# A recommendation tower on one core: GpSimd's gathers in two gated runs per tile, and the two gram fills side by side

## The chip, the cores and the metric

The kernel runs on one core of one Trainium2 chip. The metric is the device time of one execution in microseconds (us), lower is better; where several runs are given, their median is meant. The engines are called PE (TensorE, matrix products), DVE (VectorE), ACT (ScalarE), POOL (GpSimd, which here issues the indirect gathers) and SP (SyncE, which issues the plain transfers).

## What is computed

A batch of 2048 samples has 26 ids each and a dense vector of 128 numbers. Each id picks a row of 128 numbers from its table (1000 to 125000 rows). All pairs of the 27 vectors are multiplied, and the products go with the dense vector through three layers.

```
e = stack([tbl_f[ids[:, f]] for f in range(26)], axis=1)      # 2048 x 26 x 128
sd = einsum('bfd,bd->bf', e, dense)                           # 26 dot products
ss = einsum('bfd,bgd->bfg', e, e); pairs = ss[:, iu, ju]      # 325 dot products
h = concatenate([dense, sd, pairs, dense], axis=1)            # 2048 x 607
h = maximum(h @ W_top1 + b_top1, 0)                           # 512
h = maximum(h @ W_top2 + b_top2, 0)                           # 256
y = h @ W_top3                                                # 2048 x 1
```

Everything is float32.

## The kernel before

**Tiles and steps.** The 2048 samples are 16 tiles of 128. Two tiles make a step, d = tile // 2 and t = tile % 2, so there are eight steps.

**Two ways to fetch a row.** Nine small tables (`ONEHOT`) are never gathered. Their rows are looked up with matrix products: DVE writes a one-hot matrix (`set_pack`, L346), PE multiplies it by the table, which lies in SBUF split in a high and a low part (`lookup`, L592; in the first step three tables are used whole, L588). One table takes two "packs" of a step, of four products by two parts each, so a pack is 8 matmuls. Nine tables are 18 packs a step, nine in each of its two sections. In steps 3, 5 and 7 (`TEN_STEPS`) table 0 is looked up as well: 20 packs. The other tables are gathered by POOL, one indirect DMA of 128 rows for each table and tile (L311). Their 17 gathers are in groups j = 0 to 4 of 4, 4, 4, 4 and 1; a tile of the steps 3, 5 and 7 has 16 gathers and no group 4. In all 266 gathers. They land in `rows`, which has two halves, so that tile T+2 writes where tile T was.

**What is done with them.** PE transposes a group (`transpose_rows`, L605) and ACT copies it into `vecT` (`drain_rows`, L426); ACT copies a looked-up table there too (`drain_sum`, L418). When all 27 vectors of a tile are in `vecT`, PE fills two PSUM banks with the dot products of every sample with small matmuls, 64 for each half: `gram(tile, 0)` and `gram(tile, 1)`, L619, the "gram fills". ACT copies them out (`drain_gram`, L435), DVE turns and sorts them (`turn`, L356 and L362), PE transposes the result (`transpose_pairs`, L633), and then come layers 1 to 3 (L640 and L644, L653, L659).

**The order.** Every engine's order is written out by hand. On PE tile T has a "section": its gram fills first, with layer work of the step before and the first packs of the step after between them; then more packs, and after packs 2, 4, 5, 7 and 8 (counted from 0) the transposes of the groups 0 to 4 of tile T+1. A section with t = 0 holds layer 1 (three of its four parts) and half of layer 2; a section with t = 1 the rest of layer 2, layer 3 and the first part of layer 1. The first step's 18 packs stand before all sections, with the transposes of tile 0 after packs 3, 6, 9, 12 and 13. The last two tiles have an order of their own, which the change does not touch.

**The semaphores that matter.** `vec_filled` counts PE's fills of the two vector banks (transposed groups and gram halves), and `pack_done` counts the packs that PE has finished. POOL waits, before group j of tile T+2, until PE has transposed group j of tile T (the buffer is free then), and before group 3 also for both gram halves of tile T.

Of the kernel before, what the change touches and what calls it, by code (L numbers as in the profile page):

```python
# [18 lines left out]
LOOKED_UP = ONEHOT + [SOMETIMES]  # L19
TEN_STEPS = [3, 5, 7]  # L20
LATE_SPLIT = 4
GRAM_AHEAD_OF = 3
SPLIT_AT_FIRST = len(LOOKED_UP) - LATE_SPLIT


# [33 lines left out]
def build(nc, dense_t, ids, ids_t, tables, weights, y):  # L59
# [3 lines left out]
    TD = 2  # L63
# [32 lines left out]
    X_AFTER = 7  # L96
    LATE_LOW_AT = {2 * n: SPLIT_AT_FIRST + n for n in range(LATE_SPLIT)}
    SUM_AFTER = 5

    STEP_USES = TD + M1 + M2 + 1  # L100

# [3 lines left out]
    def sum_at(d, q):  # L105
        return sum(NH[:d]) + q

    def pack_at(d, p):
        return PER * sum_at(d, 0) + p

    def half_packs(d):
        return PER * NH[d] // TD if d < STEPS else PER * NH[0] // TD

    def groups(tile):
        return GROUPS - (tile // TD in TEN_STEPS)

    def rows_at(tile, j):
        return sum(groups(n) + 2 for n in range(tile)) + j

    def gram_at(tile, h):  # L120
        return rows_at(tile, groups(tile)) + h

    def same_rows(tile, j):
        return [n for n in range(tile % TD, tile, TD) if j < groups(n)]
# [16 lines left out]
    def layer3_at(d):  # L141
        return STEP_USES * (d + 1) - (d == STEPS - 2)
# [10 lines left out]
    def group(j):  # L153
        return GATHERED[FG * j:FG * (j + 1)]
# [4 lines left out]
    with ctx:  # L159
# [6 lines left out]
        def sem(name):  # L166
            return ctx.enter_context(nc.semaphore(name))
# [77 lines left out]
        vec_filled, vec_drained = sem("vec_filled"), sem("vec_drained")  # L245
# [6 lines left out]
        pack_set, pack_done = sem("pack_set"), sem("pack_done")  # L252
# [40 lines left out]
        @block.gpsimd  # L293
        def _(pool):
            nc.gpsimd.memset(ident[:], 0.0).then_inc(ident_zero, 1)
            for c in heights:
                nc.gpsimd.iota(row_i[c][:], pattern=[[1, c]], base=0, channel_multiplier=c
                               ).then_inc(rows_numbered, 1)
            pool.wait_ge(ident_zero, 1)
            nc.gpsimd.affine_select(out=ident[:], in_=ident[:], compare_op=ALU.not_equal, fill=1.0, base=0,  # L300
                                    pattern=[[-1, P]], channel_multiplier=1).then_inc(ident_set, 1)

            pool.wait_ge(ids_loaded, 16)
            for tile in range(TILES):
                for j in range(groups(tile)):
                    if tile >= TD:
                        pool.wait_ge(vec_filled, rows_at(same_rows(tile, j)[-1], j) + 1)
                    if tile >= TD and j == GRAM_AHEAD_OF:
                        pool.wait_ge(vec_filled, gram_at(tile - TD, 1) + 1)
                    for n, f in enumerate(group(j)):  # L310
                        nc.gpsimd.indirect_dma_start(  # L311
                            rows[:, tile % TD, FG * j + n, :], None, tables[f],
                            bass.IndirectOffsetOnAxis(ids_all[:, tile, f:f + 1], 0)
                        ).then_inc(gathered[tile % TD][j], 16)

        @block.vector
        def _(dve):
# [59 lines left out]
            for tile in range(TILES):  # L377
                d, t = tile // TD, tile % TD
                for k in range(half_packs(d + 1)):
# [4 lines left out]
                    if k == TURN_AFTER:  # L384
                        turn(tile)
                    if tile == 1 and k == SUM_AFTER:
                        dve.wait_ge(weights_loaded, 16)
# [4 lines left out]
        def _(act):  # L392
# [37 lines left out]
            def drain_gram(tile, h):  # L430
                use = gram_at(tile, h)
                if h == 0 and tile:
                    act.wait_ge(tile_turned, tile)
                act.wait_ge(vec_filled, use + 1)
                nc.scalar.copy(dots[:, h * HALF:(h + 1) * HALF, :],  # L435
                               vec_bank[use % 2][:, 0:HALF * GC].rearrange("p (i f) -> p i f", f=GC)
                               ).then_inc(vec_drained, 1)
# [15 lines left out]
            def drain_layer1(d, m):  # L453
                drain_unit(layer1_at(d, m), h1, m, b1_sb, 0, DS)

            def drain_layer2(d, m):
                drain_unit(layer2_at(d, m), h2, m, b2_sb, 0, DS)

            def drain_y(use, d, t0, nt):
                act.wait_ge(work_filled, use + 1)  # L460
                nc.scalar.copy(y_by_tile[:, TD * d + t0:TD * d + t0 + nt, :],
                               work_bank[use % 2][:, 0:nt * BL].rearrange("p (t i) -> p t i", t=nt)
                               ).then_inc(work_drained, 1)
# [22 lines left out]
            for tile in range(TILES - 2):  # L486
                d, t = tile // TD, tile % TD
                for h in range(2):
                    drain_gram(tile, h)
                    if t == 0 and d:  # L490
                        drain_layer1(d - 1, 1 + h)
                    if t == 1 and d and h == 0:
                        drain_layer2(d - 1, 1)
                    if t == 1 and d and h == 1:
                        drain_y(layer3_at(d - 1), d - 1, 0, TD)
                    drain_table(d + 1, half_packs(d + 1) * t + h)
                    if tile == 0 and h + 2 < LATE_SPLIT:
                        copy_whole(SPLIT_AT_FIRST + h + 2)
                        set_late_high(SPLIT_AT_FIRST + h + 2)
                for k in range(2, half_packs(d + 1)):  # L500
                    drain_table(d + 1, half_packs(d + 1) * t + k)
                    if k in ROWS_AFTER and ROWS_AFTER[k] < groups(tile + 1):
                        drain_rows(tile + 1, ROWS_AFTER[k])
                    if t == 0 and d and k == LATE_LAYER1_AFTER:
                        drain_layer1(d - 1, M1 - 1)
                    if k == PAIRS_AFTER:
                        drain_pairs(tile)
                    if t == 0 and d + 1 < STEPS and k == X_AFTER:
                        copy_x(d + 1)
                if t == 0 and d:  # L510
                    drain_layer2(d - 1, 0)
                if t == 1:
                    drain_layer1(d, 0)
# [10 lines left out]
            d = STEPS - 1  # L524
# [34 lines left out]
        def _(pe):  # L559
# [36 lines left out]
            def free_vec(use):  # L596
                if use >= 2:
                    pe.wait_ge(vec_drained, use - 1)
# [10 lines left out]
            def gram(tile, h):  # L609
                into = gram_at(tile, h)  # L610
                if h == 0:
                    pe.wait_ge(sum_drained, sum_at(tile // TD + 1, 0))
                    pe.wait_ge(x_copied, tile // TD + 1)
                    pe.wait_ge(vec_drained, rows_at(tile, groups(tile) - 1) + 1)
                free_vec(into)
                for i in range(HALF):
                    for j in range(4):
                        s = BL * j + h * HALF + i
                        last = nc.tensor.matmul(vec_bank[into % 2][BL * j:BL * j + GC, i * GC:(i + 1) * GC],  # L619
                                                vecT[:, slot(tile), s, 0:GC], vecT[:, slot(tile), s, 1:VECS],  # L620
                                                start=True, stop=True)
                last.then_inc(vec_filled, 1)
# [71 lines left out]
            for tile in range(TILES - 2):  # L694
                d, t = tile // TD, tile % TD
                for h in range(2):
                    gram(tile, h)
                    if t == 0 and d:
                        layer1(d - 1, 1 + h)
                    if t == 1 and d and h == 0:  # L700
                        layer2(d - 1, 1)
                    if t == 1 and d and h == 1:
                        layer3(d - 1)
                    table_step(d + 1, half_packs(d + 1) * t + h)
                for k in range(2, half_packs(d + 1)):
                    table_step(d + 1, half_packs(d + 1) * t + k)
                    if k in ROWS_AFTER and ROWS_AFTER[k] < groups(tile + 1):
                        transpose_rows(tile + 1, ROWS_AFTER[k])
                    if t == 0 and d and k == LATE_LAYER1_AFTER:
                        layer1(d - 1, M1 - 1)  # L710
                    if k == PAIRS_AFTER:
                        transpose_pairs(tile)
                if t == 0 and d:
                    layer2(d - 1, 0)
                if t == 1:
                    if d == 0:
                        pe.wait_ge(w1x_summed, 1)
                    layer1(d, 0)
# [22 lines left out]
            d = STEPS - 1  # L741
# [77 lines left out]
```

## Time and profile before

| | |
|---|---|
| median of 3 timed runs | 369.42 us (369.02 to 369.57) |
| span of the profiled execution | 543.7 us |
| PE busy in it | 392.0 us |
| POOL busy in it | 253.7 us |
| DVE busy in it | 233.2 us |
| ACT busy in it | 186.9 us |
| mean granted TensorE clock in it | 0.836 |

The page gives the span, from the first to the last instruction, and no time for what lies before and behind it. The profiled execution is 174 us longer than the timed ones, so its durations of single instructions can be used, while its waits have to be looked at one by one. In a timeline a row stands for neighbouring instructions of one kind: start, duration, engine, line, operation, count, and in brackets the idle time ahead with what ended it. "x8" of L592 is one pack. A float32 product of layers 1 to 3 counts as two.

### The profile page before, as it was taken

How to read it: one execution, taken by the hardware profiler on the slowest of the kernel's cores; microseconds unless marked ns; L12 is line 12 of the kernel's file. 1: busy time of each engine (PE TensorE's matmuls, PEld its weight loads, DVE VectorE, ACT ScalarE, POOL GpSimd, SP SyncE). 2: the span in 40 equal slices, each digit the busy share in tenths (PEclk: the TensorE clock that was granted, in tenths of full speed). 3: DMA queues.
4: the chain of work that ended last, by engine and by line, in shares of the span. 5: the costliest groups of instructions: out<-in, count | busy, mean ns of one | idle time of the engine just before them, and what ended most of it. 6: DMA issues, size and time to landing. Idle time of an engine off the chain costs nothing.

```text
span 543.7 us, 13728 instructions
## 1 busy us (share of the span) xinstructions
PE 392.0 (72%) x6224; PEld 342.7 (63%) x6224; DVE 233.2 (43%) x324; ACT 186.9 (34%) x283; POOL 253.7 (47%) x273
## 2 busy tenths in 40 slices
PE   5631776283986829876896959967795956969987
PEld 3520775272875718766685938857684934859876
DVE  6310887271461523635353533716454432555202
ACT  0110773231442323422324324513434313344453
POOL 6775627265263742627265363626465371552000
PEclk9955798595897958989797868979798885989999
DMA  8725105011020110201011011211112010110000
GB/s 229 204 54 128 30 20 190 26 41 43 12 59 26 46 39 17 59 21 53 23 41 53 24 43 28 58 27 45 35 41 54 20 51 17 40 49 22 2 4 2
DMA packets 11755, 26.84 MB, mean 49 GB/s; under 512 B 4652, under 2 KB 5804, under 8 KB 11570
## 3 DMA queue, kind: packets, MB, share of 16 engines
q0 software_dynamic: 8512, 17.45, 12.3%
q1 hardware_dynamic: 3186, 8.52, 5.5%
q8 instruction: 49, 0.80, 0.6%
q14 instruction: 8, 0.07, 0.0%
HBM read 25.95 MB, written 0.01 MB: 48 GB/s over the span
## 4 chain that ended last, share of the span: by engine, by line
PE 58%; another core or an unknown queue 24%; issue 10%; ACT 8%
PE sum_bank L592 22%; PE vec_bank L619 9%; PE work L644 8%; PE work L653 6%; PE vec_bank L605 5%; ACT vecT L426 4%; PE work L640 3%; ACT vecT L418 2%; PE id_bank L566 1%; PE work L633 1%; PE work L729 1%; PE work L659 0%; ACT parts L395 0%; ACT late L442 0%
## 5 line engine op out<-in xcount | busy, mean ns | idle before, releaser
L311 POOL DMA_INDIRECT rows<-in_tbl,ids_all x266 | 252.9, 951 | 245.6 <-PE vec_bank L619 143.8
L346 DVE TENSOR_TENSOR onehot<-id_bank,row_f 125x1024 fp32r<-125x1024 f32 x150 | 177.0, 1217 | 256.4 <-remote 133.7
L592 PE MATMUL sum_bank<-onehot,parts 125*128 125x256 f32 x1152 | 187.8, 306 | 54.3 <-issue 34.5
L592 PEld LDWEIGHTS sum_bank<-onehot,parts 125*128 125x128 f32 x1152 | 164.5, 204 | 67.4 <-issue 57.9
L426 ACT COPY vecT<-vec_bank 128x512 f32<-128x512 f32 (+1 forms) x74 | 83.2, 1128 | 82.1 <-remote 66.0
L418 ACT COPY vecT<-sum_bank 128x256 f32<-128x256 f32 x75 | 52.5, 700 | 118.0 <-remote 76.4
L619 PE MATMUL vec_bank<-vecT 128*26 128x26 f32 x4096 | 51.8, 200 | 45.8 <-issue 29.8
L619 PEld LDWEIGHTS vec_bank<-vecT 128*26 128x26 f32 x4096 | 45.0, 113 | 58.3 <-issue 52.5
L644 PE MATMUL work<-late,w_all 126*128 126x256 f32 (+1 forms) x192 | 51.5, 410 | 14.5 <-ACT late L442 14.5
L450 ACT ACTIVATE late<-work,w_all 128x256 f32<-128x256 f32 (+1 forms) x50 | 22.8, 458 | 95.5 <-remote 38.4
L605 PE MATMUL vec_bank<-ident,rows 128*128 128x128 f32 x266 | 45.8, 286 | 12.7 <-issue 10.9
L644 PEld LDWEIGHTS work<-late,w_all 126*128 126x128 f32 x192 | 39.2, 215 | 23.4 <-ACT late L442 17.2
L605 PEld LDWEIGHTS vec_bank<-ident,rows 128*128 128x128 f32 x266 | 32.7, 146 | 17.3 <-issue 16.5
L356 DVE STREAM_TRANSPOSE late<-late 128x832 f32<-128x832 f32 x16 | 29.3, 1830 | 25.2 <-ACT late L435 25.2
L653 PE MATMUL work<-late,w_all 128*128 128x256 f32 x112 | 35.6, 475 | 0.2 <-ACT late L450 0.2
L435 ACT COPY late<-vec_bank 128x416 f32<-128x416 f32 x32 | 16.2, 506 | 43.0 <-PE vec_bank L619 43.0
L653 PEld LDWEIGHTS work<-late,w_all 128*128 128x128 f32 x112 | 25.9, 242 | 5.1 <-ACT late L450 0.4
L640 PE MATMUL work<-xT,w_all 128*128 128x256 f32 (+1 forms) x64 | 24.2, 456 | 5.2 <-issue 5.2
L566 PE MATMUL id_bank<-idsT,pick 128*128 128x512 f32 x38 | 19.8, 526 | 6.0 <-DVE idsT L370 4.8
L362 DVE COPY late<-late 128x6 f32<-128x6 f32 (+2 forms) x144 | 16.6, 195 | 1.5
L640 PEld LDWEIGHTS work<-xT,w_all 128*128 128x128 f32 x64 | 11.8, 221 | 6.6 <-issue 5.9
L588 PE MATMUL sum_bank<-onehot,w_all 125*128 125x256 f32 x48 | 13.7, 448 | 2.0 <-DMA w_all<-in_tbl 2.0
(40 smaller groups left out, 106.3 us busy)
## 6 DMA issues: line engine op xcount, KB each, us to landing
rows<-in_tbl,ids_all POOLq DMA_INDIRECT x266
late<-in_tbl SPq DMA_DIRECT2D x7, 480.0 KB
w_all<-in_weights SPq DMA_DIRECT2D x1, 1571.0 KB
w_all<-in_tbl SPq DMA_DIRECT2D x3, 480.0 KB
xT<-in_dense_t SPq DMA_DIRECT2D x8, 128.0 KB
vecT<-in_ids_t SPq DMA_DIRECT2D x1, 256.0 KB, 2.9
late<-in_weights SPq DMA_DIRECT2D x1, 256.0 KB
ids_all<-in_ids SPq DMA_DIRECT2D x1, 208.0 KB, 2.3
```

Of the source, the lines that this page charges most:

```text
L311: nc.gpsimd.indirect_dma_start(rows[:, tile % TD, FG * j + n, :], None, tables[f], bass.IndirectOffsetOnAxis(ids_all[:, tile, f:f + 1], 0) ...
L346: nc.vector.tensor_tensor(onehot[:, use % RING, 0:width, :], bass.AP(got.tensor, got.offset, [got.ap[0], [0, width], [1, DS]]), bass.AP(nu ...
L356: nc.vector.transpose(turned.rearrange("p c i -> p (c i)"), dots.rearrange("p i c -> p c i")).then_inc(tile_turned, 1)
L418: nc.scalar.copy(step_vec(d, place(LOOKED_UP[n] + 1)), sum_bank[use % 2][:, 0:DS].rearrange("p (t s) -> p t s", t=TD)).then_inc(sum_draine ...
L426: nc.scalar.copy(vecT[:, slot(tile), :, spot:spot + n].rearrange("d s v -> d v s"), vec_bank[use % 2][:, 0:n * P].rearrange("d (v s) -> d ...
L566: nc.tensor.matmul(id_bank[pair % 2][:], bass.AP(row.tensor, row.offset, [row.ap[0], [0, P]]), idsT[:], start=True, stop=True).then_inc(id ...
L592: last = nc.tensor.matmul(into_sum, parts[:, k, CH_AT[n] + c0 + c, :], hot, start=first and k == 0, stop=final and k == PARTS - 1)
L605: last = nc.tensor.transpose(vec_bank[into % 2][:, n * P:(n + 1) * P], rows[:, tile % TD, FG * j + n, :], ident[:])
L619: last = nc.tensor.matmul(vec_bank[into % 2][BL * j:BL * j + GC, i * GC:(i + 1) * GC], vecT[:, slot(tile), s, 0:GC], vecT[:, slot(tile), s ...
L640: nc.tensor.matmul(out, w1x[:, cols], xT[:, d % 2, s0:s0 + ns], start=True, stop=False)
L644: last = nc.tensor.matmul(out, w1p[:, b, cols], pairsT[0:KP, b, s0:s0 + ns], start=False, stop=(b == KT - 1))
L653: last = nc.tensor.matmul(work_bank[use % 2][:, 0:ns], w2_sb[:, b, m * P:(m + 1) * P], h1[:, b, s0:s0 + ns], start=(b == 0), stop=(b == M1 ...
```

## The change

GpSimd no longer waits before each group. Before the first gather of tile T+2 it waits for both gram halves of tile T; before group 2 it waits until PE has finished the fifth pack of tile T's section. So a tile's gathers are one run of 8 (groups 0 and 1) and one of 9 or 8. Tile 1, which waited for nothing, gets two waits: for 8 finished packs of the first step ahead of group 0, and for 15 ahead of group 2. On PE and ACT the two gram fills, and their copies, stand side by side; what stood between them follows.

```diff
-GRAM_AHEAD_OF = 3
+SECOND_HALF_FROM = 2
...
+    HALF_WAITS_FOR = 5
+    TILE1_WAITS_FOR = [8, 15]
...
             for tile in range(TILES):
                 for j in range(groups(tile)):
-                    if tile >= TD:
-                        pool.wait_ge(vec_filled, rows_at(same_rows(tile, j)[-1], j) + 1)
-                    if tile >= TD and j == GRAM_AHEAD_OF:
+                    if tile >= TD and j == 0:
                         pool.wait_ge(vec_filled, gram_at(tile - TD, 1) + 1)
+                    if tile >= TD and j == SECOND_HALF_FROM:
+                        d, t = tile // TD, tile % TD
+                        pool.wait_ge(pack_done, pack_at(d, half_packs(d) * t) + HALF_WAITS_FOR)
+                    if tile == 1 and j == 0:
+                        pool.wait_ge(pack_done, TILE1_WAITS_FOR[0])
+                    if tile == 1 and j == SECOND_HALF_FROM:
+                        pool.wait_ge(pack_done, TILE1_WAITS_FOR[1])
...
                 for h in range(2):
                     drain_gram(tile, h)
+                for h in range(2):
                     if t == 0 and d:
                         drain_layer1(d - 1, 1 + h)
...
                 for h in range(2):
                     gram(tile, h)
+                for h in range(2):
                     if t == 0 and d:
                         layer1(d - 1, 1 + h)
```

POOL's queue before, at the start of tile 2 (a table's name in each row; tables 1 to 5 are group 0, 8 to 13 group 1, 14 and on group 2):

```order
L311 DMA rows<-in_tbl_1,ids_all 128x128 [waits vec_filled]
L311 DMA rows<-in_tbl_2,ids_all 128x128
L311 DMA rows<-in_tbl_3,ids_all 128x128
L311 DMA rows<-in_tbl_5,ids_all 128x128
L311 DMA rows<-in_tbl_8,ids_all 128x128 [waits vec_filled]
L311 DMA rows<-in_tbl_11,ids_all 128x128
L311 DMA rows<-in_tbl_12,ids_all 128x128
L311 DMA rows<-in_tbl_13,ids_all 128x128
L311 DMA rows<-in_tbl_14,ids_all 128x128 [waits vec_filled]
L311 DMA rows<-in_tbl_16,ids_all 128x128
```

Each group has its wait. The same place in the changed kernel:

```order
L318 DMA rows<-in_tbl_1,ids_all 128x128 [waits vec_filled]
L318 DMA rows<-in_tbl_2,ids_all 128x128
L318 DMA rows<-in_tbl_3,ids_all 128x128
L318 DMA rows<-in_tbl_5,ids_all 128x128
L318 DMA rows<-in_tbl_8,ids_all 128x128
L318 DMA rows<-in_tbl_11,ids_all 128x128
L318 DMA rows<-in_tbl_12,ids_all 128x128
L318 DMA rows<-in_tbl_13,ids_all 128x128
L318 DMA rows<-in_tbl_14,ids_all 128x128 [waits pack_done]
L318 DMA rows<-in_tbl_16,ids_all 128x128
```

The first wait is now for the gram of tile 0, that of group 1 is gone, and that of group 2 is for a pack.

PE's queue before, from the gram of tile 2 on (L619 gram, L640 and L644 a part of layer 1, L592 a pack):

```order
L619 MATMUL vec_bank<-vecT 26x26 [waits vec_drained,x_copied,sum_drained]
L619 MATMUL vec_bank<-vecT 26x26 x63
L640 MATMUL work<-xT,w_all 128x256 [waits work_drained]
L644 MATMUL work<-late,w_all 128x256 x3
L592 MATMUL sum_bank<-onehot,parts 128x256 [waits pack_set,sum_drained]
L592 MATMUL sum_bank<-onehot,parts 128x256 x7
L619 MATMUL vec_bank<-vecT 26x26 [waits vec_drained]
```

And in the changed kernel:

```order
L627 MATMUL vec_bank<-vecT 26x26 [waits vec_drained,x_copied,sum_drained]
L627 MATMUL vec_bank<-vecT 26x26 x63
L627 MATMUL vec_bank<-vecT 26x26 [waits vec_drained]
L627 MATMUL vec_bank<-vecT 26x26 x63
L648 MATMUL work<-xT,w_all 128x256 [waits work_drained]
L652 MATMUL work<-late,w_all 128x256 x3
L600 MATMUL sum_bank<-onehot,parts 128x256 [waits pack_set,sum_drained]
```

The second gram half has moved ahead of one part of layer 1 and one pack.

## Rows read from the trace of the kernel before

**Rows 1.** Waits of POOL: engine, line, releaser: total us, times, longest.
```profile
POOL rows L311 <- PE vec_bank L619: 143.8, 14, 14.4
```

**Rows 2.** Stretches: us busy (instructions) of PE, PEld, DVE, ACT, POOL, clock, DMA share.
```profile
177.50:186.00 8.50, 8.47 (x72) 8.21 (x70) 7.44 (x14) 3.72 (x4) 6.61 (x7) 1.00 0.18 48
186.00:202.00 16.00, 4.58 (x15) 2.50 (x15) 1.75 (x2) 1.69 (x3) 9.45 (x10) 0.65 0.18 46
500.00:541.00 41.00, 37.59 (x775) 33.45 (x774) 7.82 (x22) 20.04 (x38) 0.00 (x0) 1.00 0.02 4
```

**Rows 3.** Timeline of POOL: the gathers at the start.
```profile
3.29 1.10 POOL L311 DMA_INDIRECT rows<-in_tbl,ids_all  x1 [1.89 <-DMA ids_all<-in_ids]
4.69 0.95 POOL L311 DMA_INDIRECT rows<-in_tbl,ids_all  x1 [0.30 <-issue]
...
23.42 0.94 POOL L311 DMA_INDIRECT rows<-in_tbl,ids_all  x1 [0.30 <-issue]
...
49.64 0.94 POOL L311 DMA_INDIRECT rows<-in_tbl,ids_all  x1 [0.30 <-issue]
```

**Rows 4.** Timeline of POOL: first and last of 17 gathers in one run.
```profile
429.43 0.94 POOL L311 DMA_INDIRECT rows<-in_tbl,ids_all  x1 [9.81 <-PE vec_bank L619]
...
449.40 0.94 POOL L311 DMA_INDIRECT rows<-in_tbl,ids_all  x1 [0.30 <-issue]
```

**Rows 5.** The page's DMA issues: KB each, us from issue to landing.
```profile
ids_all<-in_ids SPq DMA_DIRECT2D x1, 208.0 KB, 2.3
```

**Rows 6.** Timeline of PE: first step and section of tile 0.
```profile
18.31 3.62 PE L588 MATMUL sum_bank<-onehot,w_all 125*128 125x256 f32 x16
27.54 2.05 PE L592 MATMUL sum_bank<-onehot,parts 125*128 125x256 f32 x8 [5.60 <-ACT vecT L418]
...
57.70 3.72 PE L592 MATMUL sum_bank<-onehot,parts 125*128 125x256 f32 x16 [6.22 <-ACT vecT L418]
...
66.57 1.18 PE L592 MATMUL sum_bank<-onehot,parts 125*128 125x256 f32 x8
...
72.86 1.27 PE L619 MATMUL vec_bank<-vecT 128*26 128x26 f32 x128 [0.75 <-ACT vecT L418]
...
92.45 0.27 PE L605 MATMUL vec_bank<-ident,rows 128*128 128x128 f32 x1
```

**Rows 7.** Timeline of PE: parts of the sections of tiles 12 and 13.
```profile
462.65 1.27 PE L619 MATMUL vec_bank<-vecT 128*26 128x26 f32 x128
...
470.77 1.30 PE L592 MATMUL sum_bank<-onehot,parts 125*128 125x256 f32 x8
471.91 0.60 PE L605 MATMUL vec_bank<-ident,rows 128*128 128x128 f32 x4
...
480.42 1.89 PE L653 MATMUL work<-late,w_all 128*128 128x256 f32 x8
...
491.88 1.30 PE L592 MATMUL sum_bank<-onehot,parts 125*128 125x256 f32 x8
...
505.57 0.59 PE L640 MATMUL work<-xT,w_all 128*128 128x256 f32 x2
```

**Rows 8.** Timeline of PE: the last transposed groups and the issue waits behind them.
```profile
521.93 1.13 PE L605 MATMUL vec_bank<-ident,rows 128*128 128x128 f32 x8
...
528.64 1.12 PE L619 MATMUL vec_bank<-vecT 128*26 128x26 f32 x111 [0.99 <-issue]
...
532.27 1.05 PE L729 MATMUL work<-late,w_all 128*128 128x128 f32 x8 [0.53 <-issue]
```

**Rows 9.** Timeline of POOL: the two longest gathers.
```profile
62.16 1.72 POOL L311 DMA_INDIRECT rows<-in_tbl,ids_all  x1 [0.30 <-PE vec_bank L605]
...
65.43 1.85 POOL L311 DMA_INDIRECT rows<-in_tbl,ids_all  x1 [0.30 <-issue]
```

**Rows 10.** Timeline of DVE: the low parts of tables at that time.
```profile
61.86 1.21 DVE L325 TENSOR_TENSOR parts<-late,parts 125x1024 fp32r<-125x1024 f32 x1
...
65.25 1.21 DVE L325 TENSOR_TENSOR parts<-late,parts 125x1024 fp32r<-125x1024 f32 x1
```

## The prediction, made before the changed kernel ran

> **What bounds the kernel now.** I began with the times: the profiled execution spans 543.7 us and the timed runs take 369.42 us, 174 us less. So the first question is which of the profile's waits exist in a timed run. POOL's waits for the gram add up to 143.8 us [rows 1], and the stretches show what stands behind them. From 177.5 to 186.0 us PE is busy without a gap at full clock (8.47 of 8.50 us); from 186 to 202 us, with POOL's gathers going on, PE issues 15 matmuls in 16 us and DVE and ACT stand still with it; from 500 us on, when the gathers are over, PE is busy for 37.59 of 41 us, again at full clock [rows 2]. So PE stalls only while gathers are under way, and only after some 9 us of them. A timed run has no room for such stalls: all of them together would be the 174 us. I take them as a thing of the recording, and come back to the opposite reading as a rival. What remains is the instructions' own durations.
>
> POOL has the longest row of these. It starts at 3.29 us and then issues a gather every (49.64 - 4.69) / 36 = 1.249 us [rows 3]. A run of 17 gathers that passes several of the old waits takes (449.40 - 429.43) / 16 = 1.248 us for each, so a wait that is already met costs nothing [rows 4]. Without a real wait POOL ends at 3.3 + 265 x 1.249 + 0.9 = 335.2 us. The last group then has to land; the nearest row is a plain load, 2.3 us [rows 5]. From the transposes of the last groups, at about 522.4 us, to the span's end are 21.3 us, of which 1.5 us are issue waits [rows 8]: 19.8 us. **POOL's floor: 335.2 + 2.3 + 19.8 = 357.3 us.**
>
> PE's floor comes from the sections. That of tile 12 (t = 0, ten packs): 19.7 us from the second gram half to the end of layer 2 at 482.3, less 0.7 us of issue waits, and 4.1 us for the gram half, layer part and pack before it, together 23.0 us. That of tile 13: 491.88 to 505.57 is 13.7 us, and with a gram half, half of layer 2 and a part of layer 1 at its two ends (4.8 us) 18.5 us [rows 7]. A pack is 1.14 us (470.77 to 471.91), so sections of nine packs take 21.9 and 17.4 us. A step is 41.5 us on PE where POOL needs 32 gathers, 40.0 us, and 39.3 us where POOL needs 34, 42.5 us. Over steps 1 to 6 PE needs 242 us and POOL 247. The two are nearly in balance, with POOL the longer. Around them stand 39.9 us to the first gram and 20.5 us for tile 0's section (both below), some 15 us for tile 1's, which has no layer 2 and 3 yet, and the tail from 505.57 + 1.8 us to the span's end, 36.3 us less the 1.5 us of issue waits. PE's floor is about 352 us. The 12 us from 357 to 369.4 are what lies around the span, for which the page has no time, and small waits.
>
> **The change, part by part.** (1) *Tile 1's first gate, 8 packs.* POOL is through with tile 0's 17 gathers at 23.42 + 1.25 = 24.7 us [rows 3]. When is the eighth pack done? The first six end at 18.31 + 3.62 = 21.9 us; the next two waited in this profile for ACT, in a stretch of stalls [rows 6]. Free of it they follow at once: 2 x 1.03 us and 0.7 us for a transposed group and an id product between them give 24.7 us; at half clock, as this profile shows the seventh (2.05 us), 26.9 us. So the gate costs POOL 0 to 2.2 us, and on the floor above each of them is a microsecond of the result. I take 0.3 us, since the clock was full up to there, and one semaphore has to arrive.
>
> (2) *Tile 1's second gate, 15 packs.* In the undisturbed stretch the ninth pack starts at 57.70 and the fifteenth ends at 66.57 + 1.0, 9.9 us later [rows 6]. The eighth ends at 24.7, so the gate opens at 34.6; the run of 8 gathers ahead of it ends at 24.7 + 8 x 1.249 = 34.7. Cost: 0, up to 0.3; it shifts with (1).
>
> (3) *The gram gate ahead of group 0.* This one is new for groups 0 and 1, which before waited only for transposes. Who is queued behind it is the whole of POOL's work. Tile 2: the first gram starts 72.86 - 57.70 = 15.2 us after the ninth pack [rows 6], at 39.9 us, and its two halves end 2.5 us later, at 42.4 us; POOL arrives at 24.7 + 0.3 + 17 x 1.249 = 46.2 us. Slack 3.8 us. Tile 3: the section of tile 0 took some 20.5 us, to just behind the last transpose at 92.45 [rows 6]; gram done at about 63 us, POOL there at 67.5 us. Slack 4.5 us. Later: where PE waits for POOL it stands in the section of tile T at the last group of tile T+1, so the gram of tile T, at the head of that section, lies behind it. The section begins some 5 us after tile T's last landing and the gram is done 2.5 us in, about 10 us after POOL left tile T; POOL comes to tile T+2 21.2 us after leaving tile T. Slack 11 us. Cost: 0.
>
> (4) *The pack gate ahead of group 2.* In a section with t = 0 the fifth pack ends 13.4 us after the section's start (471.9 against 458.5), in one with t = 1 some 9 us after. A first run that starts with the gram, 2.5 us in, ends at 12.5 us. So POOL waits 0.9 us at most, in every other tile, and only if it stood at the gram gate too; by (3) it comes 11 us later. Cost 0; the other end is 7 x 0.9 = 6 us.
>
> (5) *The waits that go.* The old waits for transposes were met when POOL arrived, and cost 0 [rows 4]. The old gram wait ahead of group 3 goes as well: 0.
>
> (6) *Gram fills side by side.* The same instructions. The second half waits only for the last group's drain, which the first half has waited for. What stood between, a layer part and a pack, comes 1.2 us later (one gram half). ACT has both copies first, 0.5 us each, and the layer's drain behind them, covered by the pack on PE. In a section with t = 1 layer 3 needs layer 2 drained: before a pack and a gram half covered that, 2.3 us, now the pack alone, 1.1 us, against about 0.5 us of ACT and the way there. 0; the ends are -0.2 us (gram done earlier) and +0.3 us for each of six steps.
>
> The sum: 369.42 + 0.3 + 0.1 + 0 = **369.8 us**. Measured against the profiled execution it would be the same 0.4 us on a span of 543.7, if that were undisturbed, which it is not: its own waits hang on the recording, so I set the sum on the median.
>
> A rule that bears on POOL's row. Two gathers took 1.72 and 1.85 us instead of 0.94 [rows 9], and both began just behind the start of a DVE subtraction that reads two SBUF operands, at 61.86 and 65.25 us [rows 10]. The Trainium skill, "SBUF — State Buffer", Who interferes with whom, says that such a DVE instruction contends with a GpSimd instruction that reads SBUF, and that whoever starts first keeps the port; the trace agrees, at 0.8 to 0.9 us for each meeting. The change moves tile 1's gathers by some tenths against six such subtractions. A meeting more or less moves the result by 0.9 us either way, and I take none.
>
> **The rivals.** *A: the stalls behind long runs of gathers are partly real.* Then 12 us between floor and time are stalls, not surroundings. In the profile stalls begin some 9 us into a run; a run of 8 gathers lasts 10 us, so two runs with a pause between them escape most of a stall that a run of 12 or 17 gets. If 6 in 10 of the 12 us go, the time is 369.4 - 7.1 = 362.3 us. For it: PE's stall in rows 2 is in step with POOL's gathers. Against it: it cannot have this size in a timed run, and on the floor POOL has no pause between its runs. The same page of the Trainium skill says that a DMA does not contend with a compute engine; no timed run here shows it, and by that rule this rival gives 369.8.
>
> *B, the other side: POOL's start gates bind.* It decides when the eighth pack ends later than 24.7 us. At the half-clock pace it ends at 26.9, and the fifteenth at 36.8, when the first run is just through: +2.2 us on everything behind, and with 0.3 for the semaphores 369.4 + 2.5 = 371.9 us. For it: PE had gaps in the first 15 us and the table loads go on. Against it: the clock was full when the sixth pack ended.
>
> *C: PE is the bound and the gathers are ready anyway.* Then no gate matters and only (6) is left: 369.4, within 0.3 us.
>
> **How the numbers follow.** Forecast 0.40 (369.8, own range 369.0 to 370.8), C 0.13, B 0.25, A 0.22. A measurement of this kernel can tell about 0.2% from no change, 0.74 us. Faster: 0.22 from A and 0.07 from fewer meetings with DVE in the forecast and C, 0.29. Slower: 0.25 from B and 0.09 from the upper end of the forecast, 0.34. Within: 0.37. The range runs from 363.5, into A, to 373.0, behind B with part of the pack gate's 6 us.
>
> **What would show it.** In the profile after: POOL's first gather of tile 1 starts within 0.5 us of 24.7 us, if PE is not stalled by then, and gathers stay at 1.25 us. PE's sections have the same sums, gram halves 1.2 us apart. The waits of POOL are split between the gram and the packs; the recorded stalls get shorter, since the runs are, and so may the span, without the timed runs following. I am wrong if the timed runs follow the span (A), or if a kernel without tile 1's gates is faster by more than 1 us (B).

## The result: 5% slower, and all of it where the gram fills touch

The changed kernel takes 388.00 us (median of 4 runs, 386.61 to 388.25), the kernel before 369.22 us beside it. The ratio is 1.052, with a 95% interval of 1.049 to 1.054. I had forecast 369.8 us, in a range of 363.5 to 373.0. Now and then an execution of any kernel ran in a slower state, at a lower granted clock; medians and ratios here leave such executions out.

The profile of the changed kernel has a span of 386.4 us; the same execution was timed at 388.24 us. This recording is not disturbed as the one of before was, so the two cannot be laid side by side. A second profile of the kernel before ("before again", below) has a span of 368.2 us; it is the one to compare with. The page of the changed kernel:

```profile
span 386.4 us, 13714 instructions
PE 346.4 (90%) x6224; PEld 315.5 (82%) x6224; DVE 230.3 (60%) x324; ACT 189.2 (49%) x283; POOL 256.9 (66%) x273
PE 81%; issue 8%; POOL 4%; DMA 3%; DVE 2%; ACT 1%; DVEq 0%
L627 PEld LDWEIGHTS vec_bank<-vecT 128*26 128x26 f32 x4096 | 43.9, 103 | 34.4 <-issue 31.8
```

And of before again:

```profile
PE 343.8 (93%) x6224; PEld 313.0 (85%) x6224; DVE 230.7 (63%) x324; ACT 188.8 (51%) x283; POOL 256.9 (70%) x273
PE 76%; POOL 10%; issue 6%; DMA 4%; ACT 2%; DVE 1%; POOLq 0%; ACTq 0%
L619 PEld LDWEIGHTS vec_bank<-vecT 128*26 128x26 f32 x4096 | 44.2, 103 | 20.5 <-issue 14.6
```

PE has the same work; in the changed kernel it is idle for 40.0 us instead of 24.4. The last row of each is the gram fill, and behind the bar stands the idle time ahead of its weight loads: waits that no semaphore explains ("issue") have grown from 14.6 to 31.8 us.

The timeline of PE shows where. First the head of the section of tile 6 in the changed kernel (answering to [rows 7], where the halves stood apart):

```profile
170.62 2.68 PE L627 MATMUL vec_bank<-vecT 128*26 128x26 f32 x185
175.03 0.79 PE L627 MATMUL vec_bank<-vecT 128*26 128x26 f32 x71 [1.74 <-issue]
175.75 0.70 PE L648 MATMUL work<-xT,w_all 128*128 128x256 f32 x2
176.28 2.65 PE L652 MATMUL work<-late,w_all 126*128 126x256 f32 x6
178.37 1.96 PE L600 MATMUL sum_bank<-onehot,parts 125*128 125x256 f32 x8
```

Then the same section in before again:

```profile
161.35 1.80 PE L619 MATMUL vec_bank<-vecT 128*26 128x26 f32 x128
163.09 0.70 PE L640 MATMUL work<-xT,w_all 128*128 128x256 f32 x2
163.62 1.46 PE L644 MATMUL work<-late,w_all 126*128 126x256 f32 x6
164.73 1.30 PE L592 MATMUL sum_bank<-onehot,parts 125*128 125x256 f32 x8
165.97 1.65 PE L619 MATMUL vec_bank<-vecT 128*26 128x26 f32 x128
```

A half's 64 matmuls stand in a trace as 128 records, a pair of halves as 256, each with a weight load. The pair takes 175.82 - 170.62 = 5.2 us side by side and 1.80 + 1.65 = 3.5 us apart. Here 185 of the 256 run, then PE stands still for 1.7 us with nothing to wait for. All 14 pairs of the changed kernel have one such stall, of 0.3 to 1.7 us. Where in the pair it comes differs: after 219 records in tile 2, after 130 in tile 13.

```profile
79.63 3.47 PE L627 MATMUL vec_bank<-vecT 128*26 128x26 f32 x219
84.67 0.67 PE L627 MATMUL vec_bank<-vecT 128*26 128x26 f32 x37 [1.57 <-issue]
...
326.88 1.82 PE L627 MATMUL vec_bank<-vecT 128*26 128x26 f32 x130
329.38 1.25 PE L627 MATMUL vec_bank<-vecT 128*26 128x26 f32 x126 [0.68 <-issue]
```

The layer part behind tile 6's pair is slower too: its 6 records take 2.65 us instead of 1.46. The stretches of the changed kernel show why (columns as in [rows 2]):

```profile
173.30:175.00 1.70, 0.00 (x0) 0.00 (x0) 0.00 (x0) 0.12 (x1) 1.35 (x2) 1.00 0.17 43
175.80:181.00 5.20, 5.20 (x22) 4.53 (x21) 0.00 (x0) 0.98 (x2) 3.77 (x4) 0.67 0.21 54
```

Behind the idle stretch the granted clock is 0.67 on average, a part at the 1.2 GHz level. That is so right behind the stalls of tiles 2 and 6, and not behind most of the others: PE's busy time grows by 2.6 us in all, its issue waits in the gram fills from 2.7 to 16.9 us.

Between the first gram and the last lies the whole difference. From the first gram to the last, tile 0 to tile 15, before again and changed:

```profile
39.62 1.81 PE L619 MATMUL vec_bank<-vecT 128*26 128x26 f32 x128 [0.75 <-ACT vecT L418]
...
349.50 1.26 PE L619 MATMUL vec_bank<-vecT 128*26 128x26 f32 x128 [0.20 <-ACT vecT L426]
```

```profile
38.62 2.82 PE L627 MATMUL vec_bank<-vecT 128*26 128x26 f32 x174 [0.76 <-ACT vecT L425]
...
367.98 1.26 PE L627 MATMUL vec_bank<-vecT 128*26 128x26 f32 x128 [0.22 <-ACT vecT L433]
```

That is 309.9 against 329.4 us, 19.5 us more for 14 pairs, 1.4 us each; start and tail are the same within a microsecond. Stalls in the 14 pairs are 14.5 us of it (16.1 against 1.6), PE's longer busy time is 2.6; the rest was not taken apart.

GpSimd's waits in the changed kernel, then in before again:

```profile
POOL rows L318 <- PE vec_bank L627: 8.8, 6, 3.0
POOL rows L318 <- PE sum_bank L600: 6.2, 4, 2.8
```

```profile
POOL rows L311 <- PE vec_bank L605: 2.4, 8, 0.3
POOL rows L311 <- PE vec_bank L619: 0.6, 2, 0.3
```

The 143.8 us of [rows 1] were indeed a thing of the recording: undisturbed, GpSimd waits for PE 3.0 us in all. In the changed kernel it waits 15 us, on the new gates; whether that is cause or consequence is the first question.

### The profile page after: what moved, and what is told of

The parts are those of the page before. It is cut to its first block, busy times and chain, and to the rows that moved or that the text cites. A ratio compares the mean times of both kernels' runs of the same rounds, so it can differ in the third digit from the quotient of the medians.

```text
span 386.4 us, 13714 instructions
## 1 busy us (share of the span) xinstructions
PE 346.4 (90%) x6224; PEld 315.5 (82%) x6224; DVE 230.3 (60%) x324; ACT 189.2 (49%) x283; POOL 256.9 (66%) x273
## 4 chain that ended last, share of the span: by engine, by line
PE 81%; issue 8%; POOL 4%; DMA 3%; DVE 2%; ACT 1%; DVEq 0%
PE sum_bank L600 33%; PE vec_bank L627 13%; PE work L652 11%; PE work L661 7%; PE vec_bank L613 7%; POOL rows L318 4%; PE work L648 4%; DMA rows<-in_tbl,ids_all 2%; PE id_bank L574 2%; PE work L641 1%; PE work L738 1%; DVE onehot L353 1%; PE work L667 1%; DMA ids_all<-in_ids 1%; DVE parts L338 1%
## 5 line engine op out<-in xcount | busy, mean ns | idle before, releaser
L318 POOL DMA_INDIRECT rows<-in_tbl,ids_all x266 | 256.1, 963 | 94.8 <-issue 77.7
L600 PE MATMUL sum_bank<-onehot,parts 125*128 125x256 f32 x1152 | 168.9, 293 | 1.4 <-issue 0.9
L600 PEld LDWEIGHTS sum_bank<-onehot,parts 125*128 125x128 f32 x1152 | 151.8, 193 | 5.7 <-issue 2.1
L433 ACT COPY vecT<-vec_bank 128x512 f32<-128x512 f32 (+1 forms) x74 | 84.8, 1149 | 16.9 <-PE vec_bank L613 16.4
L425 ACT COPY vecT<-sum_bank 128x256 f32<-128x256 f32 x75 | 52.5, 700 | 42.4 <-PE sum_bank L600 28.5
L627 PE MATMUL vec_bank<-vecT 128*26 128x26 f32 x4096 | 52.8, 192 | 22.1 <-issue 16.9
L627 PEld LDWEIGHTS vec_bank<-vecT 128*26 128x26 f32 x4096 | 43.9, 103 | 34.4 <-issue 31.8
L652 PE MATMUL work<-late,w_all 126*128 126x256 f32 (+1 forms) x192 | 46.1, 377 | 0.0
L613 PE MATMUL vec_bank<-ident,rows 128*128 128x128 f32 x266 | 41.7, 275 | 0.7 <-DMA rows<-in_tbl,ids_all 0.7
L652 PEld LDWEIGHTS work<-late,w_all 126*128 126x128 f32 x192 | 36.1, 196 | 5.1
L661 PE MATMUL work<-late,w_all 128*128 128x256 f32 x112 | 28.4, 398 | 2.1 <-issue 1.9
L661 PEld LDWEIGHTS work<-late,w_all 128*128 128x128 f32 x112 | 20.8, 195 | 5.3 <-issue 2.3
L648 PE MATMUL work<-xT,w_all 128*128 128x256 f32 (+1 forms) x64 | 19.8, 391 | 0.0
L596 PEld LDWEIGHTS sum_bank<-onehot,w_all 125*128 125x128 f32 x48 | 10.5, 223 | 5.0 <-issue 3.2
```

The source lines that it names most:

```text
L318: nc.gpsimd.indirect_dma_start(rows[:, tile % TD, FG * j + n, :], None, tables[f], bass.IndirectOffsetOnAxis(ids_all[:, tile, f:f + 1], 0) ...
L425: nc.scalar.copy(step_vec(d, place(LOOKED_UP[n] + 1)), sum_bank[use % 2][:, 0:DS].rearrange("p (t s) -> p t s", t=TD)).then_inc(sum_draine ...
L433: nc.scalar.copy(vecT[:, slot(tile), :, spot:spot + n].rearrange("d s v -> d v s"), vec_bank[use % 2][:, 0:n * P].rearrange("d (v s) -> d ...
L600: last = nc.tensor.matmul(into_sum, parts[:, k, CH_AT[n] + c0 + c, :], hot, start=first and k == 0, stop=final and k == PARTS - 1)
L613: last = nc.tensor.transpose(vec_bank[into % 2][:, n * P:(n + 1) * P], rows[:, tile % TD, FG * j + n, :], ident[:])
L648: nc.tensor.matmul(out, w1x[:, cols], xT[:, d % 2, s0:s0 + ns], start=True, stop=False)
```

## The experiments

Two theories stood after the result. *The fills:* side by side they make PE stall. *The gates:* GpSimd is held up, and PE with it.

### The gates alone, the fills alone

Gates alone (label gates_split): the changed kernel, with the old order on PE and ACT.

```diff
                 for h in range(2):
                     gram(tile, h)
-                for h in range(2):
                     if t == 0 and d:
                         layer1(d - 1, 1 + h)
```

> The changed kernel with all its gates on GpSimd, but with the gram fills where they were before (a layer part and a pack between the two halves). Theory 1, the side-by-side fills cost: in the changed kernel a pair of gram halves takes about 5 us with an issue gap of 1 to 1.7 us in it, where two separate halves take 2 x 1.25 us; taken apart the halves lose the gap, some 2.5 us for each of 14 tiles, and the time falls from 388 to between 366 and 372 us. Theory 2, the gates cost: the time stays at 385 to 389 us.

Measured: 368.73 us; ratio to before 0.9992, interval 0.9966 to 1.0017. All the gates together cost and bring nothing that can be told, and GpSimd's waits on them shrink from 15 to 1.7 us:

```profile
POOL rows L318 <- PE sum_bank L599: 1.1, 2, 0.8
POOL rows L318 <- PE vec_bank L612: 0.6, 2, 0.3
```

So the 15 us were a consequence.

Fills alone (before_adjacent): the kernel before, with the same line put in.

> The kernel before with its own gates, and only the gram fills and their copies moved side by side. Theory 1: 384 to 392 us, with the issue gap in each pair. Theory 2: 368 to 371 us, since only gates would matter.

Measured: 385.42 us (median of 2), ratio 1.044 (1.038 to 1.049). Its profile is of a longer execution (span 390.6 us), so only the shape is read from it: tile 6's pair again runs 185 records, waits 1.04 us, and runs 71. The fills are the cause, the gates are not.

### Tile 1's gates taken out

after_free_start is the changed kernel without these lines:

```diff
-                    if tile == 1 and j == 0:
-                        pool.wait_ge(pack_done, TILE1_WAITS_FOR[0])
-                    if tile == 1 and j == SECOND_HALF_FROM:
-                        pool.wait_ge(pack_done, TILE1_WAITS_FOR[1])
```

> The changed kernel without the two gates of tile 1. The eighth pack ended at about 23.8 us in the changed kernel, when tile 0's gathers were through, so both theories that look elsewhere expect 387 to 389 us; a cost of the start gates (rival B of the prediction) would show as 1 us or more less.

Measured: 389.82 us (median of 3), ratio 1.061 (1.054 to 1.067). Not faster; rival B is out. In the changed kernel's own timeline of POOL the seventeenth gather and tile 1's first stand back to back:

```profile
24.39 1.84 POOL L318 DMA_INDIRECT rows<-in_tbl,ids_all  x1 [0.30 <-issue]
26.54 0.94 POOL L318 DMA_INDIRECT rows<-in_tbl,ids_all  x1 [0.30 <-issue]
```

### The kernel before once more

before_again is the kernel before without an edit.

> The kernel before once more, for a profile. If the recorded stalls of the first profile (543.7 us) are a thing of the recording, another profile may have a span near the timed 369 us. Then the gathers should run without a wait of more than a few us from 3.3 us to about 345 us if GpSimd is the bound, and the sections on PE should contain small waits for gathered rows.

Measured: 369.98 us in its one run, span 368.2. The expectation held for GpSimd: no real wait from 3.5 us on, last gather at 339.38 us. PE's waits for gathered rows are 2.4 us in all, fewer than I expected, and PE is busy for 93% of the span: neither engine has much room.

### Are the gathers part of it?

nogather_split and nogather_adjacent issue gathers for tiles 0 and 1 alone; the second has the fills side by side.

```diff
-            for tile in range(TILES):
+            for tile in range(TD):
                 for j in range(groups(tile)):
...
-                pe.wait_ge(gathered[tile % TD][j], 16 * len(group(j)) * (len(same_rows(tile, j)) + 1))
+                pe.wait_ge(gathered[tile % TD][j], 16 * len(group(j)))
```

> The kernel before without the gathers of tiles 2 to 15 (232 of 266 left out; later tiles reuse the rows of tiles 0 and 1, so the result is not the reference's). PE then waits for no gathered row. If GpSimd alone sets the time before, it falls by 10 us or more, to below 359 us; the section sums of the prediction put PE's own floor at about 352 us. If PE is as much of a bound, it stays at 364 to 368 us.

> The same without those gathers, with the gram fills side by side. Theory F (PE's own instruction supply runs dry in a burst of 512 short instructions): the gap in each pair stays at 1 us or more and the time is 15 to 30 us above the run with the fills apart. Theory G (the gathers' descriptors delay the supply or the operands): without them the gap shrinks to below 0.4 us and the two runs differ by less than 5 us.

Measured: 356.98 us apart (0.969, 0.964 to 0.973) and 382.11 us side by side (median of 3; 1.039, 1.034 to 1.044). The cost of the side-by-side fills is 25 us here, more than the 19 us with gathers. The pairs of tiles 2 and 6 without gathers:

```profile
79.86 2.04 PE L620 MATMUL vec_bank<-vecT 128*26 128x26 f32 x219
83.97 0.50 PE L620 MATMUL vec_bank<-vecT 128*26 128x26 f32 x37 [2.06 <-issue]
...
168.60 1.76 PE L620 MATMUL vec_bank<-vecT 128*26 128x26 f32 x185
172.72 0.79 PE L620 MATMUL vec_bank<-vecT 128*26 128x26 f32 x71 [2.36 <-issue]
```

Again 219 and 185 records, then a gap. In tile 6 it is now 2.4 us, and the pair lasts 4.9 us against 5.2. In every one of the 14 pairs the stall stands before the same matmul as in the changed kernel, whatever the gathers do. PE runs the first 185 faster and waits longer for the rest, so the end comes at nearly the same time. That is what a supply with a pace of its own looks like, and not a delay made by the gathers. Theory G is out. One thing was not expected: without gathers a half that stands alone is faster.

```profile
155.33 1.27 PE L619 MATMUL vec_bank<-vecT 128*26 128x26 f32 x128
```

1.27 us instead of 1.80 and 1.65. PE's busy time in the gram fills is 42.4 us here and 53.9 us in before again. These 11.5 us, some 0.9 us for each tile, are what the gathers cost PE in the kernel before, and they are about the size of the 12 us by which this run is faster. Row by row the trace of before again shows the cost as short pauses within a half: 59 of 0.13 to 0.28 us between two neighbouring gram matmuls, 58 of them 0.36 to 0.44 or 1.12 to 1.24 us after a gather's start and the last at 0.97. Without the later gathers 6 are left.

### How much must stand between the halves

pack_between leaves the pack between them and moves only the layer part behind the second half. The diff is abridged: the words in brackets stand for code.

```diff
-                for h in range(2):
-                    gram(tile, h)
-                    (layer part h)
-                    table_step(d + 1, half_packs(d + 1) * t + h)
+                for what, h in [("gram", 0), ("pack", 0), ("gram", 1), ("layer", 0), ("pack", 1), ("layer", 1)]:
+                    (what it says)
```

> The kernel before with only the layer part moved behind the second gram half; the pack stays between the halves (0.95 us of work in 16 short-of-nothing instructions). Theory F: what counts is the time between the halves in which few instructions are used; 2.7 us of it was nearly enough, none costs 20 us, 1 us should leave a gap of 0.3 to 0.9 us in a pair and a time of 374 to 383 us. If instead it counts only whether the halves touch, the time is that of before, 369 us.

Measured: 372.59 us, ratio 1.009 (1.006 to 1.013), a little below the range. With 2.8 us of other work between the halves a pair mostly costs nothing extra (before again has a gap in 4 of 14 pairs, 1.6 us in all). With about 1 us the gaps run from none to 1.1 us (tile 6 below), with none from 0.3 to 1.7:

```profile
165.87 0.60 PE L626 MATMUL vec_bank<-vecT 128*26 128x26 f32 x48
166.85 1.37 PE L626 MATMUL vec_bank<-vecT 128*26 128x26 f32 x80 [0.38 <-issue]
```

### Half of the matmuls

half_fill_adjacent has the fills side by side, but fills each bank by half (ACT's copy is changed to match, not shown).

```diff
-                for i in range(HALF):
+                for i in range(HALF // 2):
                     for j in range(4):
```

> The fills side by side, but each with half of its matmuls (the dot products of 8 of 16 samples in a group are left out and the others copied twice, so the result is not the reference's). A pair is then as many instructions as one half is before. Theory F: no issue gap over 0.4 us in a pair, and a time below the 369 us of before by about 1.25 us of PE work for a tile or what GpSimd allows of it, 355 to 366 us. If a pair of fills as such stalls PE (a bank or a drain), the gap stays over 1 us.

Measured: 363.1 us in its one run, and no issue gap in a pair (128 records in 1.8 to 2.1 us). Two banks filled one after the other do not stall PE; the number of instructions does. Here PE waits for gathered rows instead, so this is about what GpSimd alone needs:

```profile
PE vec_bank L607 <- DMA rows<-in_tbl,ids_all: 17.2, 14, 2.4
```

### An idle microsecond between them

If the supply refills at its own pace, a pause should serve as well as other work. wait_between puts one into the changed kernel:

```diff
                 free_vec(into)
+                if h == 1 and tile < TILES - 2:
+                    pe.wait_ge(vec_drained, into)
```

> The changed kernel with one wait more: the second gram half of a tile waits until ACT has copied out the first, about 1 us in which PE does nothing and uses no instruction. Theory F (the supply of instructions runs dry and fills up at its own pace): the wait takes the place of the issue gap, which falls from 1.1-1.7 us to below 0.9, and the time stays within 1% of the changed kernel's 388 us. Theory H (a fixed stall that comes with the second half of a pair, whatever stands before it): the wait is added to the gap, 14 x 1 us, and the time is 398 to 404 us.

Measured: 387.36 us (median of 3), within 1 us of the changed kernel; ratio to before 1.055 (1.049 to 1.062). Its timeline and PE's waits:

```profile
173.38 0.62 PE L629 MATMUL vec_bank<-vecT 128*26 128x26 f32 x53 [0.76 <-ACT late L442]
174.58 0.82 PE L629 MATMUL vec_bank<-vecT 128*26 128x26 f32 x75 [0.58 <-issue]
```

```profile
PE vec_bank L629 <- ACT late L442: 13.3, 14, 1.4
PE vec_bank L629 <- issue: 8.8, 11, 1.6
```

PE now waits 13.3 us for ACT, and its issue gaps fell from 16.9 to 8.8 us. The wait took the place of about half of the gaps' time; three gaps are still over the 0.9 us that I expected. The 5 us more of idle time in all did not lengthen the kernel. The granted clock, 0.995 in this profile and 0.982 in that of the changed kernel, may be why. Theory H, which asked for 10 us more, is out.

What is supplied late? The page of the changed kernel has a queue that carries nothing but instructions:

```profile
q8 instruction: 49, 0.80, 0.8%
```

49 packets with 0.80 MB together are 16 KB each, and PE's 12448 records (matmuls and weight loads) make 254 for each packet. A pair of halves is 512 records, so it eats about two packets in 2.5 us, where a pack eats a sixteenth of one in 1 us. The Trainium skill, "Runtime: NRT & Kernel Launch", Instruction fetch mechanics, says that the instruction memory is refilled in 16 KiB blocks of 256 instructions, by a queue that the sequencer drives; the packets agree. It also calls the cost mostly hidden; here it is not, and the measurement decides.

No row names this queue as releaser, but the traces hold the time of each of its packets and every instruction of PE. Take the twelve recordings other than the disturbed first one, and count PE's records from the first one on (matmuls, weight loads, waits on semaphores). They have 91 issue stalls over 0.25 us in gram fills, in eleven of the twelve (none in half_fill_adjacent), and all 91 stand at a record whose number leaves 193 when divided by 256: the stalls come where a block of 256 instructions ends. The place at record 449 goes with the queue's first packet, that at 705 with its second, and so on: each of the 91 stalls ends 1.2 to 1.6 us after the end of its packet, and no such place, stalled or not, is passed sooner than 1.2 us behind its packet. For tile 6 of the changed kernel the packet runs from 172.61 to 173.48 us, and PE goes on at 175.03. Two packets of this queue never start less than 3.3 us apart, while a block of gram instructions alone lasts 1.3 us. So PE does wait for its next block of instructions. It also explains the place of the stall: from one pair to the next are some 768 instructions, three blocks, so the block's end moves through the pair slowly, from record 219 in tile 2 to 130 in tile 13.

### The other direction

spread cuts each half in two and puts a layer part or a pack between any two quarters; spread_ten also looks up table 0 with matmuls in step 2.

```diff
+    [("first", 0), ("layer", 0), ("second", 0), ("pack", 0), ("first", 1), ("layer", 1), ("second", 1), ("pack", 1)]
...
-TEN_STEPS = [3, 5, 7]
+TEN_STEPS = [2, 3, 5, 7]
```

> The kernel before with the other extreme: each gram half is cut in two quarters, with a layer part or a pack between any two of them, so that no run of short matmuls is longer than 128 instructions. Theory F: the halves of before still lose some 0.5 us each to supply while gathers run (1.8 against 1.27 us without gathers); in quarters that loss goes, up to 1 us for each of 14 tiles on PE, but GpSimd's last gather still starts at 339 us, so of the 369 us 0 to 4 us can go: 365 to 369 us. If the slower halves come from contention for the operands and not from supply, cutting them changes nothing: 368.5 to 370 us.

> As spread, and step 2 looks up table 0 with matmuls as the steps 3, 5 and 7 do: 2 gathers fewer for GpSimd (2.5 us less before its last one) and 2 packs more for PE (1.9 to 2.3 us). If GpSimd is what bounds the spread kernel, 1.5 to 2.5 us faster than it; if PE is, 1 to 2 us slower than it.

Measured: spread 366.81 us, ratio 0.9952 (0.9923 to 0.9980), half a percent faster than before and the best version here. spread_ten 369.95 us, 1.0028 (1.0005 to 1.0050), 3 us slower than spread, more than the 1 to 2 us expected: two packs cost PE more than two gathers save, so PE is the nearer bound. Tile 6's quarters take 0.99, 0.73, 0.73 and 0.73 us by their rows, and of the 59 short pauses of before again 22 are left. The gain in time is small all the same.

## Why the prediction was wrong

**The step that failed is (6), the fills side by side.** I sized it at 0, with ends of -0.2 us and +0.3 us for each of six steps. It measured 1.4 us for each of 14 tiles, 19.5 us. I costed the same instructions at the same sum of durations, looked at the semaphores that each waits for, and did not ask whether PE gets 512 instructions in 2.5 us. It does not: it waits for a block of 256 in every pair.

**The row that said so was on the table.** In [rows 8] the second half of tile 15's gram, at 528.64 us, has an issue wait of 0.99 us. There a layer part of 1.0 us was all that stood between the halves, the gathers had been over for 28 us, and the clock was full: a stretch that I had called undisturbed. I subtracted that wait from the tail as recording. It stands in the undisturbed profiles too, in before again:

```profile
351.77 0.31 PE L619 MATMUL vec_bank<-vecT 128*26 128x26 f32 x17
353.20 1.12 PE L619 MATMUL vec_bank<-vecT 128*26 128x26 f32 x111 [1.12 <-issue]
```

A wait of 1 us with 1.0 us of spacing would have priced no spacing at some 1 us for each of 14 pairs, an estimate, as the wait also depends on where the block ends. Right as it was that the 174 us were the recording's, that reading made me throw out every issue wait with it.

**What bounds the kernel** was nearly right. GpSimd needs no wait: confirmed by before again, where it waits 3 us. Its floor was 357.3 us; half_fill_adjacent, where PE waits for rows, spans 361.3. The last gather starts at 339.4 us and not at 334.3, because six gathers at the start meet a DVE subtraction (1.41 to 1.85 us instead of 0.94, 4.9 us in all); I had named the mechanism from [rows 9, 10] and counted none. PE's floor of about 352 us is a span of 354.0 in nogather_split. But the 12 us between floor and time were not surroundings: these are 1.8 us (369.98 against a span of 368.2). On GpSimd's side 5 us of the rest are the slow gathers at the start; on PE's side it is mostly the gathers' pauses in the gram fills.

**(1) to (5), the gates:** right. Zero was forecast apart from 0.4 us at the start, and gates_split is at 0.9992. Tile 1's first gather starts at 26.54 us in the changed kernel and not within 0.5 us of 24.7, but two slow gathers ahead of it made it late, not the gate; the 0.3 us were not there either. The 0.1 us in the sum belongs to no term of the list. That GpSimd does wait 15 us on the gates in the changed kernel comes from (6), which makes PE late.

**Rival A** (gathers stall PE in timed runs as well) was half right in kind: the gathers do slow PE, by 0.9 us a tile, in pauses of some 0.2 us and not by long stalls. Runs of 8 and 9 instead of 12 to 17 gathers don't change that, so its 362.3 us was wrong. **Rival B** was wrong. **Rival C** put PE as the bound with (6) at nothing: the first half was the better reading of this kernel, and the second failed with (6). No rival had the mechanism that decided.

## What to carry to other kernels

A run of many short instructions has a price beside their durations: count the instructions that an engine must take in per microsecond, and leave longer work between two such runs. Here 256 in 1.3 us mostly passed and 512 in 2.5 us did not; a block of 256 came at best every 3.3 us. An idle time without a releaser that stands before the same instruction in kernel after kernel is a sign to look at the instruction queue. When a disturbed profile makes you discount idle time, discount it by stretch: a gap that stands where the disturbance cannot reach is the kernel's own.

## What the runs showed of the hardware

- PE's instructions arrive in packets of 16 KB, one for each 256 instructions. In twelve recordings all 91 stalls over 0.25 us in the gram fills stand at the end of such a block, and PE goes on 1.2 to 1.6 us after the block's packet has ended. Side by side, 256 matmul records with as many weight loads stalled for 0.3 to 2.0 us with gathers (one pair had no stall) and for 1.2 to 2.7 us without; 2.8 us of longer work in between removed most stalls.
- The clock fell to the 1.2 GHz level right behind two of the changed kernel's 14 stalls; its mean is 0.982 there and 0.995 in before again.
- While gathers were issued, 128 records of the gram fill took 1.65 to 1.80 us in tile 6; without them 1.27 us. PE pauses for 0.13 to 0.28 us at two set times of a gather, about 0.4 and 1.15 us after its start. These pauses keep to the gathers and not to the instruction blocks. What PE waits for in them is open.
- Five or six of GpSimd's gathers in the first 40 us took 1.25 to 2.00 us instead of 0.94 in every undisturbed profile, each started while a DVE subtraction of two SBUF operands ran.
- The same kernel was recorded once with a span of 543.7 us and once with 368.2 us, while its timed runs kept to 369.
